# Moving the application of a layer norm from VectorE to ScalarE in two feed-forward stages

## The reference, cut to what matters

```python
def _layernorm(x, axis=-1, eps=1e-05):
    m = jnp.mean(x, axis=axis, keepdims=True)
    v = jnp.var(x, axis=axis, keepdims=True)
    return (x - m) / jnp.sqrt(v + eps)

def _L0_ffn_ref(x, base_w, base_b, lora_A, lora_B, router_w, router_b):
    result = jnp.einsum('bsd,od->bso', x, base_w) + base_b
    logits = jnp.einsum('bsd,ed->bse', x, router_w) + router_b
    gating = jax.nn.softmax(logits, axis=-1).astype(jnp.bfloat16)
    mid = jnp.einsum('bsd,dr->bsr', x, lora_A)
    lora_out = jnp.einsum('bsr,erd,bse->bsd', mid, lora_B, gating.astype(jnp.float32))
    return result + lora_out * SCALING

x = x + 0.5 * _L0_ffn_ref(_layernorm(x, axis=-1), ...)
x = x + _L0_attn_ref(_layernorm(x, axis=-1), ...)
x = x + 0.5 * _L0_ffn_ref(_layernorm(x, axis=-1), ...)
...
```

## Time and profile before

| what | value |
|---|---|
| time, median of 3 executions | 1731.96 us (1723.12 to 1746.84) |
| the profiled execution: its time, its span | 1735.6 us, 1733.8 us |
| `ffn1`, first statistics to end of last residual | 8.5 to 56.0 us |
| `ffn2`, the same | 473.5 to 533.2 us |
| busy over the span: PE, DVE, ACT, POOL | 89%, 67%, 47%, 46% |
| granted clock of TensorE, mean over the span | 0.911 |

### The profile page before, as it was taken

One profiled execution on the slowest core, in us unless ns is written; L12 is line 12 of the kernel. 1 busy time (PEld: TensorE's weight loads), 2 busy tenths in 40 slices (PEclk: granted clock), 3 DMA queues, 4 the chain that ended last, 5 costly groups with the idle time before them and its releaser, 6 DMA issues. The chain is left out here.

```text
span 1733.8 us, 36975 instructions
## 1 busy us (share of the span) xinstructions
PE 1537.2 (89%) x10054; PEld 1258.9 (73%) x10054; DVE 1167.2 (67%) x4550; ACT 815.3 (47%) x1995; POOL 796.3 (46%) x1129
## 2 busy tenths in 40 slices
PE   6699999999897757999959999999999686699995
PEld 5477777777587546888847888887888574588884
DVE  6448888888575743555548898988898666255554
ACT  2247777777625213444424555555555431244442
POOL 2246666666524240222217786877787504111111
PEclk9759999999956778999979999999999868899998
DMA  4598000000023010001021111111111001000003
GB/s 126 149 300 225 0 0 0 0 0 0 7 80 116 18 37 14 27 26 27 27 72 42 41 38 38 37 37 37 37 37 38 1 2 37 25 26 27 25 27 110
DMA packets 101116, 82.91 MB, mean 48 GB/s; under 512 B 9820, under 2 KB 88351, under 8 KB 100720
## 3 DMA queue, kind: packets, MB, share of 16 engines
q1 hardware_dynamic: 95178, 69.87, 15.1%
q0 software_dynamic: 4416, 9.58, 1.6%
q10 hardware_dynamic: 1382, 1.83, 0.4%
HBM read 23.71 MB, written 40.75 MB: 37 GB/s over the span
## 5 line engine op out<-in xcount | busy, mean ns | idle before, releaser
L892 DVE SCALAR_TENSOR_TENSOR moe_block_act<-banks,moe_taken,moe_block_gated 128x128 f32<-128x128 f32 x592 | 166.8, 344 | 186.4 <-ACT moe_block_gated L936 179.1
L921 POOL DMA_INDIRECT y_rows<-moe_block_y,moe_taken x74 | 71.4, 965 | 383.2 <-ACT moe_block_y L946 383.2
L1181 DVE CUSTOM_DVE_ANT_0 attn_z<-banks,rel_bias 128x128 f32<-128x128 f32 (+1 forms) x512 | 161.9, 353 | 69.9 <-PE banks L1311 63.1
L1229 POOL TENSOR_TENSOR attn_z<-attn_top,attn_z 128x256 f32<-128x256 f32 x256 | 159.3, 630 | 94.2 <-DVE attn_top L1181 93.4
L1706 ACT ACTIVATE ret_normed<-banks,ret_head_shift,ret_head_rstd 128x128 f32<-128x128 f32 x256 | 103.9, 458 | 157.0 <-DVE ret_head_shift L1620 157.0
L936 ACT ACTIVATE moe_block_gated<-banks 128x512 f32<-128x512 f32 x148 | 88.6, 599 | 159.2 <-PE banks L977 159.0
L993 PE MATMUL banks<-moe_down,moe_block_actT 128*128 x1184 | 156.3, 275 | 0.0
L1258 ACT ACTIVATE attn_prob<-banks 128x384 f32<-128x384 f32 x256 | 125.9, 492 | 50.2 <-PE banks L1318 40.2
L1318 PE MATMUL banks<-ident,attn_z 128*128 128x128 f32 x768 | 144.0, 299 | 0.3 <-ACT attn_z L1253 0.3
L993 PEld LDWEIGHTS banks<-moe_down,moe_block_actT 128*128 128x128 f32 x1184 | 143.8, 192 | 0.3
L975 PE MATMUL banks<-moe_hi,moe_block_x_hi 128*128 x296 | 130.8, 442 | 1.6 <-DVE moe_block_x_lo L882 1.5
(11 more groups left out here) (260 smaller groups left out, 4255.4 us busy)
## 6 DMA issues: line engine op xcount, KB each, us to landing
slots<-moe_pad SPq DMA_DIRECT2D x12, 2304.0 KB, 20.0
ret_twins<-ret_twins SPq DMA_DIRECT2D x256, 64.0 KB, 2.0
moe_taken<-slots SPq DMA_DIRECT2D x74, 72.0 KB, 1.8
moe_back<-y_rows SPq DMA_DIRECT2D x16, 256.0 KB, 5.0
moe_stage<-in_moe_w SPq DMA_DIRECT2D x4, 576.0 KB, 7.1
bias_reversed<-scratch SPq DMA_DIRECT2D x1, 2048.0 KB, 9.6
out<-x_res SPq DMA_DIRECT2D x8, 256.0 KB, 4.5
ret_stage<-in_ret_w SPq DMA_DIRECT2D x16, 96.0 KB, 2.2
```

What stands on the lines that cost most here:

```text
L892: last = dve.scalar_tensor_tensor(act_f[:, i, at], ps_u[:, i, at], taken[:, b % RB, column:column + 1], gated[:, i, at], ALU.mult, ALU.mult)
L1181: last = dve.tensor_tensor_reduce(out=z[:, k % Z, cols], in0=ps_s[:, k % 2, cols], in1=bias, scale=1.0, scalar=-3.0e38, op0=ALU.add, op1=A ...
L1229: pool.tensor_tensor(z[:, k % Z, P:WIDTH], top[:, k % Z, 1:2].to_broadcast([P, WIDTH - P]), z[:, k % Z, P:WIDTH], ALU.subtract).then_inc(s ...
```

## The change

`normalise` goes from DVE to ACT. In its place DVE issues one small instruction a group, which computes `shift = -mean * rstd` for the group's four tiles (128x4), and ACT applies `Identity(x * rstd + shift)`, four instructions a group, as the first stage of its list. ACT's wait is now for `shift_done`. DVE's `residual`, which overwrites `x_res`, gets a wait for ACT's `xn_ready`.

```diff
-            def normalise(it, u):
+            def shift_of_mean(it, u):
                 p = u % 2
-                xg = x_group(it, u)
                 dve.wait_ge(rstd_done, count(it, u))
-                wait_free(dve, xn_transposed, count(it, u, 2))
-                for j in range(GROUP):
-                    last = dve.tensor_scalar(xn[:, p, j, :], xg[:, j, :], mv[:, p, j, 0:1], rstd[:, p, j:j + 1],
-                                             ALU.subtract, ALU.mult)
-                last.then_inc(xn_ready, 1)
+                dve.scalar_tensor_tensor(shift[:, p, :], mv[:, p, :, 0], -1.0, rstd[:, p, :], ALU.mult, ALU.mult).then_inc(shift_done, 1)
...
             def residual(it, u):
                 dve.wait_ge(y_ready, count(it, u))
+                dve.wait_ge(xn_ready, count(it, u))
...
             software_pipeline(dve, GROUPS // U, U, [
-                (3, normalise), (2, router_shift), (4, layernorm), (2, gates), (0, residual)])
+                (3, shift_of_mean), (2, router_shift), (4, layernorm), (2, gates), (0, residual)])
...
         @block.scalar
         def _(act):
+            def normalise(it, u):
+                p = u % 2
+                xg = x_group(it, u)
+                act.wait_ge(shift_done, count(it, u))
+                wait_free(act, xn_transposed, count(it, u, 2))
+                for j in range(GROUP):
+                    last = act.activation(xn[:, p, j, :], xg[:, j, :], ACT.Identity, bias=shift[:, p, j:j + 1], scale=rstd[:, p, j:j + 1])
+                last.then_inc(xn_ready, 1)
...
             software_pipeline(act, GROUPS // U, U, [
-                (2, exponent), (3, copy_xT), (1, copy_omT)] + beside(act, 0))
+                (3, normalise), (2, exponent), (3, copy_xT), (1, copy_omT)] + beside(act, 0))
```

More of the change, by code:

```diff
@@ L97, in ffn_lora_phase @@
         var_eps = sb("var_eps", [P, 2, GROUP])
+        shift = sb("shift", [P, 2, GROUP])
         xn = sb("xn", [P, 2, GROUP, C])
@@ L115, in ffn_lora_phase @@
         stats_done, aggr_done, rstd_done, xn_ready = sem("stats_done"), sem("aggr_done"), sem("rstd_done"), sem("xn_ready")
-        eps_added = sem("eps_added")
+        eps_added, shift_done = sem("eps_added"), sem("shift_done")
         ones_ready, xn_transposed, xnT_ready, small_ready = sem("ones_ready"), sem("xn_transposed"), sem("xnT_ready"), sem("small_ready")
```

## The result

The changed kernel takes **1790.16 us** (median of 4 runs, 1786.15 to 1796.46), the kernel before 1739.4 us in the same session (1723.12 to 1755.15, 4 runs). The ratio is **1.0366, 95% interval [1.0318, 1.0413]**: slower. (Executions of this kernel fall into a faster and a slower state, whatever the edit, and ratios are taken from the faster one alone, so they need not be the quotient of the medians, and where too few executions were in it none is given.) The prediction was 1734 us, 1720 to 1749, with 0.02 on slower. The profiled execution has a span of 1787.2 us and a time of 1789.29 us, against 1733.8 and 1735.6 us before: some 53.5 us are to be found between the two profiles (the medians differ by 50.8 us).

What follows compares the result with a forecast made beforehand. The prediction took PE to bound both stages. Exposed starts cost 2 us and the middle 0, giving 1735.6 + 2 = 1737.6 us on the profiled execution and 1732 + 2 = 1734 us on the median, range 1720 to 1749 us.

Steps and rivals of the forecast that it cites:

- C: Rival: `Identity` and `Exp` alternating on ACT need table loads in each group, +41 us, 1777 us; chance 0.01.
- a pattern of the clock that lasts into the later stages: Case of PE's clock pattern changing beyond the two stages, in either direction; no size given, chance 0.09.
- Group 0's transposes: Start of `ffn1`: PE's first transposes come 0.63 us later, as ACT's four activations take longer than DVE's instructions.
- group 2's: Start of `ffn1`: group 2's transposes come 1.34 us later, made of two exposed ways from statistics to PE.
- The ring in the middle: Middle of the stages: ACT-DVE loop of 3.84 us stays hidden behind PE's 4.06 us step; cost 0, ends -0.5 and +1.5 us.
- A to C: Three rivals: every group pays, +10 us (0.12); DVE was the bound, about 1 us faster (0.08); table loads, +41 us (0.01).
- D, the clock: Rival: `ffn1` stays at PE's lower pace, steps of 7.02 instead of 4.06 us, +15 us; treated as scatter.
- an earlier rise in `ffn2`: Other side of the clock rival: PE's clock rises early in `ffn2`, -15 us; treated as scatter.
- The stages' cost: Exposed starts of `ffn1` and `ffn2`, 0.7 to 1.34 us each, 1.3 to 2.7 us in sum, taken as 2 us slower.

Runs made afterwards that it cites:

- before_shift60: Kernel before, with 58 tiny memsets ahead of DVE's first work, so DVE's attention loop begins 60 instructions later, at 399: 1689.35 us, ratio 1.0017.
- before_shift106: Kernel before, with 104 tiny memsets ahead of DVE's first work, so DVE's attention loop begins 106 instructions later, at 445: 1753.13 us, ratio 1.0367.
- before_act38: Kernel before, with 38 one-column copies on ACT after its first loads, DVE's code untouched: 1715.18 us, ratio 1.0138.
- after_shift22: Changed kernel, with 20 memsets ahead of DVE's first work and 22 at the start of `ffn2`, attention loop back at 339: 1742.23 us, no ratio.
- before_shift234: Kernel before, with 232 tiny memsets ahead of DVE's first work, so DVE's attention loop begins 234 instructions later, at 573: 1779.21 us, ratio 1.0277.
- after_shift64: Changed kernel, with 62 tiny memsets ahead of DVE's first work, so DVE's attention loop begins at 381: 1695.3 us, ratio 1.0014.
- before_actlate38: Kernel before, with 38 one-column copies on ACT where it was idle, just before attention's first copy: 1735.32 us, ratio 1.0027.

## Why the prediction was wrong

**The step that failed** is a sentence of its first paragraph: "What the change can move outside them is only when the next stage starts and at what clock PE enters it." The change also moves where the next stage's code lies, and on that path came 51.2 of the 53.5 us. The same omission is in "No transfer is moved; none hangs on these engines here": the program's own transfers did not move, but the one by which DVE gets its instructions did. No rival covered it, and the highest time with a mechanism for it was C's 1777 us, by table loads that did not come (the number of loads is two, as forecast). The chance of 0.09 for a pattern of the clock that lasts into the later stages names a part of what happened, but with no cause and no price.

The row that could have warned was on the page all along: q14, marked "instruction", with 80 packets of 8 KB. With it go two questions that the trace of before answers: are there such packets inside a loop (in attention none between 158.5 and 446.4 us, so its loops were held; in retention some 11 a turn, so some were not), and how many instructions does the change take from the code ahead.

The Trainium skill has the rule as well (Runtime: NRT & Kernel Launch, Instruction fetch mechanics): a taken branch to a page that is not in the engine's window forces a fetch before execution goes on. The trace agrees (5.34 us of "issue" one step into the loop, with a packet at 155.8 us in them). It gives the page as 256 instructions and two of them held, and calls the crossing of a page's end mostly hidden. Here the measurement decides: the packets on this queue are 8 KB, the fast stretch is at most 105 places long and not 211, and attention takes 47 to 69 us more of some 400 (next paragraph).

**Where the size comes from.** The fetches stop DVE for at least the 12.7 us that stand under "issue" in six pauses. PE's clock multiplies this. Against kernels whose clock rose equally early in attention (before_shift60, 389.0 us) the changed kernel lost 457.7 - 389.0 = 68.7 us: PE was busy 49.3 us longer for the same matmuls (mean clock 0.85 against 0.97) and idle 19.4 us longer. With an equally late rise (131.3 and 130.9 us), before_shift106 lost 453.9 - 406.5 = 47.4 us against before: 39.0 busy, 8.4 idle. Most of the price is the lower clock that follows a short pause. That the pause brings the lower clock is read from their order, six times of six in the changed kernel; no experiment separates the two.

**Right, point by point.** Group 0's transposes came 0.77 us later and group 2's 1.49 us later (forecast 0.63 and 1.34), with PE released by ACT. DVE waited for PE's router matmuls 7.8 us in `ffn1`, before 0.6 us, as forecast. The ring in the middle hidden behind PE's 4.06 us step: shown in `ffn1`; in `ffn2` PE waited once for `xn`, 0.55 us at 570.85, behind ACT's cast of the weights. 64 activations at 480 ns (measured 482, median) and 16 small DVE instructions (158 ns): as forecast. A to C didn't occur. D, the clock, did not occur in `ffn1` with the change (PE's rise came at some 31 us instead of 28), but it was a real one: before_act38, after_shift22 and before_shift234 show it in their profiles. Its other half, an earlier rise in `ffn2`, did: the granted clock was back at 1.00 some 37 us after the stage's first statistics instead of 50, and the stage took 55.9 us (526.3 to 582.2) instead of 59.7. The stages' cost, forecast as 2 us, was +1.5 us in `ffn1` in the profile; for both stages together no cost was measured, with an interval of -0.3 to +0.6% (after_shift64).

**What stays open.** How many blocks DVE holds, and which one it drops, was not observed; "four held, the next one fetched ahead" is a reading of the 8 KB packets, five a turn, and of where the fast stretch ends. Nor was the period of 128. The view of waits does not always name the fetch: in before_shift106 no pause as long as 1 us is put down to "issue", and the ones that end at 226.07 and 228.42 us (2.60 and 1.17) are put down to PE, which was itself waiting for DVE at 226.77 and 229.12; the packets, at 224.0, 226.4 and 228.8 us, stand at these pauses as in the changed kernel. In before_act38 PE missed its rise in `ffn1` with a start 3.5 us later, but in after_shift22 and before_shift234 it missed it with first statistics at 8.6 and 8.7 us, where before had 8.5. So the late start is not shown to be the cause, and what decides it stays open.

## What to carry to other kernels

When an edit adds or removes instructions in front of a rolled loop, count that loop's instructions for each engine: one near the size that the engine holds (here 302 on DVE) may be fetched anew in each turn, or not, by where it begins. Compare the instruction queue's packets before and after, first of all; if a stage slows down whose code wasn't touched, move its code by a few dozen idle instructions before explaining anything else. And judge a local edit with the layout held fixed (as 1.0014 here), since a loss or gain of 3 to 4% by layout drowns what the edit itself does.

## What was not expected of the hardware

- A layout effect on DVE of 3 to 4% of the kernel (ratios 1.0277 to 1.0367 in four kernels with the old arithmetic or half the change), with starts at 339, 381 and 399 free of it and 317, 423, 445 and 573 not.
- Pauses of 1.4 to 1.5 us on DVE (five of the six) were followed by stretches in which PE ran without gaps at the lower level of its clock: from 220 to 250 us at 0.62 in the mean, with 163 matmuls in the place of 246.
- Retention, whose loop has 467 instructions on DVE and 312 on ACT, has packets in every turn in all kernels, and its length is the same, 383.1 us with 11 packets a turn before and 382.1 us with 6 after. Here the five that go with ACT's place cost nothing that shows.
- The time at which the clock rises at the start of attention differs between profiles, with no pattern in the edits that shows: at some 130 us in the profile of before (attention 406.5 us) and at some 90 us in those of the change, before_shift60 and before_actlate38 (the latter two 389 us). That is 17 us that come and go between profiles, and that a comparison of two single profiles would put down to a change.
